# Feed-forward tiles turned by transposing DMAs, PSUM taken two banks at a time, weights transposed by numpy

## The reference, cut to what matters

```python
# x (4, 512, 512) float32, 2048 tokens of D = 512; token_ids choose one of 4 experts; ctx (4, 512, 512) holds their weights
h = layernorm(x)
for e in range(4):                       # only the tokens of expert e keep its y
    g = silu(h @ ctx[e].T); u = h @ ctx[e].T        # Wg = Wu = Wd = ctx
    y = (g * u) @ ctx[e].T
x1 = x + tanh(g_xattn[0]) * y
def bit_linear(x, w, b):                 # x rounded to 8 bits by its row's largest value, w to -1, 0, 1
    gamma_x = clip(max(abs(x), -1), 1e-5);  x_dq = clip(round(x * 127 / gamma_x), -128, 127) * gamma_x / 127
    gamma_w = clip(mean(abs(w)), 1e-5);     w_dq = clip(round(w / gamma_w), -1, 1) * gamma_w
    return x_dq @ w_dq.T + b
n = layernorm(x1)
z = silu(bit_linear(n, gate_w, gate_b)) * bit_linear(n, val_w, val_b)      # hidden size H = 2048
out = x1 + tanh(g_ffn[0]) * bit_linear(z, out_w, out_b)
```

## Time and profile before

| | |
|---|---|
| median of 3 runs | 369.0 us (368.78 to 369.78) |
| the profiled execution | 367.59 us, of which its span in the profile is 365.5 us |
| stage 1, up to the first expert product | 0 to 24 us |
| stage 2, expert units | 24 to 165 us |
| stage 3, feed-forward | 165 to 365.5 us |
| PE busy | 328.6 us (90%) |
| DVE busy | 294.5 us (81%) |
| POOL busy | 259.4 us (71%) |
| ACT busy | 229.5 us (63%) |
| granted TensorE clock, mean | 0.984 of full speed |

### The profile page before, as it was taken

The page is one execution under the profiler, slowest core; times in us unless marked ns, Lnnn a source line. Parts: engine busy times, 40 slices in busy tenths (PEclk is TensorE's granted clock), DMA queues, the critical chain, the costliest instruction groups (busy, mean ns, idle before and its releaser), DMA issues.

```text
span 365.5 us, 7169 instructions
## 1 busy us (share of the span) xinstructions
PE 328.6 (90%) x1976; PEld 177.8 (49%) x1992; DVE 294.5 (81%) x644; ACT 229.5 (63%) x327; POOL 259.4 (71%) x306
## 2 busy tenths in 40 slices
PE   2858899989998999789779999999999999999972
PEld 2734455546565555454335455544555455554440
DVE  5874777767787866788999899998999889998760
ACT  2837474657874456474467776687766877668650
POOL 2470366568878887847887888888888888888711
PEclk9979999999999999999999999999999999999997
DMA  6969257569312227231101101111011110110011
GB/s 244 302 225 388 57 208 266 179 203 248 126 58 65 84 84 275 70 89 34 32 2 29 59 31 58 58 30 58 29 58 55 31 58 29 59 47 11 29 39 49
DMA packets 24598, 37.03 MB, mean 101 GB/s; under 512 B 4543, under 2 KB 12735, under 8 KB 24320
## 3 DMA queue, kind: packets, MB, share of 16 engines
q1 hardware_dynamic: 20256, 23.38, 20.4%
q0 software_dynamic: 4320, 13.40, 10.6%
HBM read 28.35 MB, written 9.20 MB: 103 GB/s over the span
## 4 chain that ended last, share of the span: by engine, by line
PE 51%; POOL 17%; issue 10%; DVE 10%; DMA 6%; ACT 4%; POOLq 1%; SPq 0%; ACTq 0%; DVEq 0%
PE bank L587 25%; PE bank L605 15%; POOL raw L349 6%; PE bank L503 4%; PE bank L595 4%; POOL x_sb L331 3%; ACT tern L705 2%; POOL xg L302 2%; DMA x_rows<-x_sb,scatter_at 2%; POOL rstd L331 2%; DMA raw<-in_ctx 2%; POOL x_rows L315 1%; PE bank L469 1%; POOL var_eps L328 1%; POOL raw L388 1%
## 5 line engine op out<-in xcount | busy, mean ns | idle before, releaser
L587 PE MATMUL bank<-tern,raw 128*128 128x512 bf16 x512 | 118.2, 379 | 1.0 <-DVE raw L1042 0.7
L388 POOL TENSOR_TENSOR raw<-raw 128x512 f32<-128x512 f32 x63 | 80.3, 1278 | 21.5 <-ACT raw L776 18.1
L503 PE MATMUL bank<-w_hi,turned 128*128 x304 | 73.8, 386 | 9.1 <-DVE turned L915 7.9
L587 PEld LDWEIGHTS bank<-tern,raw 128*128 (+1 forms) x512 | 48.7, 98 | 55.3 <-ACT raw L761 1.3
L776 ACT ACTIVATE raw<-raw 128x512 f32<-128x512 f32 x64 | 39.9, 624 | 47.8 <-DVE raw L1042 46.3
L605 PE MATMUL bank<-tern,raw 128*128 128x512 bf16 x241 | 57.1, 379 | 3.7 <-ACT raw L780 1.9
L1042 DVE SCALAR_TENSOR_TENSOR raw<-bank,raw 128x512 f32<-128x512 f32 x64 | 47.6, 744 | 6.1 <-PE bank L587 5.4
L1050 DVE SCALAR_TENSOR_TENSOR raw<-bank,raw 128x512 f32<-128x512 f32 x64 | 47.6, 744 | 3.0 <-POOL raw L388 0.9
L503 PEld LDWEIGHTS bank<-w_hi,turned 128*128 128x128 f16 x304 | 29.8, 98 | 38.9 <-issue 13.8
L768 ACT ACTIVATE raw<-raw,magic 128x1024 f32 (+1 forms) x32 | 39.2, 1235 | 6.7 <-DVE raw L1069 6.7
L713 ACT ACTIVATE sign_sb<-raw,magic 128x1024 bf16<-128x1024 f32 (+1 forms) x24 | 27.2, 1148 | 25.9 <-POOL raw L349 25.7
(11 more groups left out here) (115 smaller groups left out, 477.4 us busy)
## 6 DMA issues: line engine op xcount, KB each, us to landing
raw<-x_rows SPq DMA_DIRECT2D x16, 257.5 KB, 2.6
raw<-in_ctx SPq DMA_DIRECT2D x4, 1024.0 KB, 8.2
raw<-in_L_ffn_gate_w SPq DMA_DIRECT2D x4, 1024.0 KB, 9.8
raw<-in_L_ffn_val_w SPq DMA_DIRECT2D x4, 1024.0 KB, 5.1
raw<-in_L_ffn_out_w SPq DMA_DIRECT2D x16, 256.0 KB
raw<-in_L_ffn_gate_b SPq DMA_DIRECT2D x1, 1024.0 KB
raw<-in_L_ffn_val_b SPq DMA_DIRECT2D x1, 1024.0 KB
xg<-in_x,gather_at POOLq DMA_INDIRECT x19, 3.8
```

The source lines that it names most:

```text
L388: nc.gpsimd.tensor_tensor(flat(z[:, bass.ds(t % 2, 1), c * D:(c + 1) * D]), s_post[:, c % 2, :], v_pre[:, c % 2, :], ALU.mult).then_inc(z_ ...
L503: last = nc.tensor.matmul(acc[:, :], a[:, k * P:(k + 1) * P], flat(w[:, bass.ds(e4 + k, 1), :]), start=(k == 0 and i == 0), stop=(k == KD ...
L587: last = nc.tensor.matmul(ps[c % 2][:, :].rearrange("p (a b) -> p a b", b=P), flat(xiT[:, bass.ds(t % 2, 1), k * P:(k + 1) * P]), rhs, sta ...
```

## The change

- The host lays out the expert matrices and the three weight matrices transposed, each as 128 rows of contiguous data. The 64 expert transposes, and `turn_pair` with `keep_pair` for the 24 pairs, are gone. `w_high` and `w_low` work on pairs of 128x1024 straight from the loaded data in SBUF, all on ACT and DVE, and `sign_pair` writes `tern` directly. Each expert gets at least one unit of slots.
- Rounding begins two slots earlier (`W_SLOT` 6 in place of 8), and three tiles are loaded early in place of two (`EARLY`).
- x and z are turned by `dma_start_transpose` on SP's queue, from SBUF to SBUF: one of 128x512 for each tile's x and two of 128x1024 for its z. `x_keep`, `z_keep` and the PE transposes of stage 3 are gone.
- The gate has two places of two PSUM banks, the value one place of two banks. `gate` and `val` run 8 matmuls into 128x1024, and `pre_gate`, `pre_val`, silu, POOL's multiply (`z_pair`) and `z_max` take 1024 columns at a time, in two chunks for each tile.
- The second half of `unshift_z` moves from POOL to ACT. x of tile `t + 2` in place of `t + 1` is prepared in slot `t`.
- z and its rounded and turned forms lie where the expert weights were (`w_both`), so POOL waits for the last expert product before the first `z_pair`.
- The loops of SP, POOL and DVE over the tiles are written out. PE and ACT keep theirs.

```diff
-    EARLY = 2
+    XR = 8
+    EARLY = 3
     BEFORE_EARLY = UNITS - 3
-    W_SLOT = 8
+    W_SLOT = 6
...
-        w_hi = sb("w_hi", [P, E * KD, D], f16)
-        w_lo = sb("w_lo", [P, E * KD, D], f16)
+        w_both = sb("w_both", [P, E * KD * D], f32)
+        w_hi, w_lo = (w_both[:, i * E * KD * D // 2:(i + 1) * E * KD * D // 2].bitcast(f16).rearrange("p (n d) -> p n d", d=D)
+                      for i in range(2))
...
+        g_sb = area(2 * 2 * D).rearrange("p (b d) -> p b d", b=2)
...
+        xiT = area(D, bf16).rearrange("p (b k m) -> p b k m", b=2, m=P)
...
+        area = areas_of(w_both[:, :])
+        z = area(2 * H).rearrange("p (b d) -> p b d", b=2)
         zq = area(H)
         zi = area(H // 2, bf16)
         ziT = area(H // 2, bf16).rearrange("p (h m) -> p h m", m=P)
...
-        g_ps, v_ps = bank[0:2], bank[2:4]
-        ziT_ps = wT_ps
-        xiT_ps = bank[6][:, :].bitcast(bf16)[:, 0:D]
-        o_ps = bank[7]
+        g_ps = (banks[:, 4:6, :], banks[:, 0:2, :])
+        v_ps = banks[:, 6:8, :]
+        o_ps = bank[2]
...
+                if n == 8:
+                    sp.wait_ge(whi_made, E * KD // 2)
+                    sp.wait_ge(wlo_made, E * KD // 2)
+                w = (gate_w, val_w, out_w)[m]
+                sp.dma_start(flat(raw[:, m * G + 4 * q:m * G + 4 * q + 4, :]), w[:, q * H:(q + 1) * H]).then_inc(raw_loaded[n], 16)
...
+            def turn_x(t):
+                sp.wait_ge(xi_made, t + 1)
+                if t >= 2:
+                    sp.wait_ge(v_done, 2 * (t - 1))
+                sp.dma_start_transpose(xiT[:, t % 2, :, :], xi).then_inc(x_turned, 16)
...
+            def turn_z(t, half):
+                sp.wait_ge(zi_made[half], t + 1)
+                if t >= 1:
+                    sp.wait_ge(z_read[half], t)
+                sp.dma_start_transpose(ziT[:, half * G // 2:(half + 1) * G // 2, :],
+                                       zi[:, half * H // 2:(half + 1) * H // 2]).then_inc(z_turned[half], 16)
...
+            turn_x(0)
+            turn_x(1)
...
+            for t in range(TILES + 1):
+                if 3 <= t < TILES - 1:
+                    load_tokens(t + 1)
+                if t >= 1:
+                    turn_z(t - 1, 0)
+                    turn_z(t - 1, 1)
+                if t + 2 < TILES:
+                    turn_x(t + 2)
+                if t + XT < TILES:
+                    load_rows(t + XT)
...
+            def unshift_z(t):
+                pool.wait_ge(zq_made[0], t + 1)
+                if t >= 1:
+                    pool.wait_ge(z_turned[0], 16 * t)
+                nc.gpsimd.tensor_scalar(zi[:, 0:H // 2], zq[:, 0:H // 2], magic[:, 1:2], one[:, 0:1],
+                                        ALU.add, ALU.mult).then_inc(zi_made[0], 1)
+            def z_pair(t, c, width=2 * D):
+                pool.wait_ge(s_made, 2 * t + c + 1)
+                pool.wait_ge(v_made, 2 * t + c + 1)
+                nc.gpsimd.tensor_tensor(z[:, t % 2, 2 * D * c:2 * D * c + width], g_sb[:, c, 0:width],
+                                        v_sb[:, c, 0:width], ALU.mult).then_inc(z_made, 1)
...
+            pool.wait_ge(bias_scaled, 1)
             add_bias(0)
             add_bias(1)
...
+            pool.wait_ge(y_done, UNITS)
+            for t in range(TILES):
+                if t >= 1:
+                    z_pair(t - 1, 1)
+                if t >= 3:
+                    store(t - 3)
+                if 1 <= t < TILES - 1:
+                    add_bias(t + 1)
+                if t >= 1:
+                    unshift_z(t - 1)
+                z_pair(t, 0)
+            z_pair(TILES - 1, 1, D)
+            for t in range(TILES - 3, TILES):
+                store(t)
...
+            def gate(t, c, start=False):
+                n = 2 * t + c
+                if not start:
+                    pe.wait_ge(g_made, n - 1)
+                for b in range(2):
                     for k in range(KD):
...
+            def val(t, c, start=False):
+                n = 2 * t + c
+                if not start:
+                    pe.wait_ge(v_made, n)
+                for b in range(2):
+                    for k in range(KD):
+                        last = nc.tensor.matmul(v_ps[:, b, :], flat(xiT[:, bass.ds(t % 2, 1), k, :]),
+                                                tern[:, G + k * HC + 2 * c + b, :], start=(k == 0), stop=(k == KD - 1))
+                last.then_inc(v_done, 1)
...
+                pe.wait_ge(z_turned[half], 16 * (t + 1))
                 if half == 0 and start:
+                    pe.wait_ge(signed, PAIRS)
+                    pe.wait_ge(gu_made, UNITS)
                 elif half == 0:
                     pe.wait_ge(o_made, t)
                 for k in range(half * G // 2, (half + 1) * G // 2):
...
+                    last = nc.tensor.matmul(o_ps, ziT[:, k, :], tern[:, 2 * G + k, :],
                                             start=(k == 0), stop=(k == G - 1))
+                    if k == G // 2 - 1:
+                        last.then_inc(z_read[0], 1)
...
+            def ffn_slot(t, downs=True, start=False, start_down=False):
+                pe.wait_ge(x_turned, 16 * (t + 1))
+                gate(t, 0, start)
+                val(t, 0, start)
+                if downs:
                     down(t - 2, 0, start_down)
+                gate(t, 1, start)
+                val(t, 1)
+                if downs:
                     down(t - 2, 1)
...
+            pe.wait_ge(signed, G)
+            ffn_slot(0, downs=False, start=True)
+            ffn_slot(1, downs=False)
             ffn_slot(2, start_down=True)
             with pe.Fori(3, TILES - 1) as t:
                 ffn_slot(t)
...
+            t = TILES - 1
+            pe.wait_ge(x_turned, 16 * (t + 1))
+            gate(t, 0)
+            val(t, 0)
+            gate(t, 1)
+            val(t, 1)
+            for t in range(TILES - 3, TILES):
+                down(t, 0)
                 down(t, 1)
...
+            def w_high(p):
+                if p % 2 == 0:
+                    act.wait_ge(ctx_loaded[p // 2], 16)
+                nc.scalar.activation(flat(w_hi[:, 2 * p:2 * p + 2, :]), flat(raw[:, 2 * G + 2 * p:2 * G + 2 * p + 2, :]),
+                                     ACT.Copy, scale=W_SCALE).then_inc(whi_made, 1)
+            for p in range(E * KD // 2):
+                w_high(p)
...
+                nc.scalar.activation(flat(tern[:, bass.ds(2 * p, 2), :]), flat(raw[:, bass.ds(2 * p, 2), :]), ACT.Sign,
...
+            def unshift_z(t, start=False):
+                act.wait_ge(zq_made[1], t + 1)
+                if not start:
+                    act.wait_ge(z_turned[1], 16 * t)
+                nc.scalar.activation(zi[:, H // 2:H], zq[:, H // 2:H], ACT.Identity, bias=magic[:, 1:2]).then_inc(zi_made[1], 1)
...
+            def silu_gate(t, c):
+                act.wait_ge(g_made, 2 * t + c + 1)
+                nc.scalar.activation(g_sb[:, c, :], g_sb[:, c, :], ACT.Silu).then_inc(s_made, 1)
...
+            def ffn_slot(t, before=True, start=False, after=True):
+                silu_gate(t, 0)
                 if before:
...
+                    z_round(t - 1, 1, start)
+                    unshift_z(t - 1, start)
+                silu_gate(t, 1)
+                if after:
+                    x_round(t + 2)
+                    x_unshift(t + 2)
...
+            def w_low(p):
+                dve.wait_ge(whi_made, p + 1)
+                v.scalar_tensor_tensor(flat(w_lo[:, 2 * p:2 * p + 2, :]), flat(raw[:, 2 * G + 2 * p:2 * G + 2 * p + 2, :]), W_SCALE,
+                                       flat(w_hi[:, 2 * p:2 * p + 2, :]), ALU.mult, ALU.subtract).then_inc(wlo_made, 1)
...
+            for t in range(TILES):
+                pre_gate(t, 0)
+                if t >= 1:
+                    z_max(t - 1, 1)
+                    z_max_both(t - 1)
                     z_gamma(t - 1)
                     z_scales(t - 1)
+                pre_val(t, 0)
+                if t + 2 < TILES:
+                    tile_norm(t + 2)
+                    x_max(t + 2)
+                    x_gamma(t + 2)
+                pre_gate(t, 1)
+                if t + 2 < TILES:
+                    x_scales(t + 2)
                 z_max(t, 0)
...
+                pre_val(t, 1)
+                if 2 <= t < TILES - 1:
+                    finish(t - 2)
...
+            t, last = TILES - 1, slice(D, 2 * D)
+            dve.wait_ge(s_made, 2 * TILES)
+            dve.wait_ge(v_made, 2 * TILES)
+            v.tensor_tensor(z[:, t % 2, H - D:H], g_sb[:, 1, last], v_sb[:, 1, last], ALU.mult).then_inc(z_last, 1)
+            finish(t - 2)
+            dve.wait_ge(z_last, 1)
+            z_max(t, 1)
+            z_max_both(t)
+            z_gamma(t)
+            z_scales(t)
+            finish(t - 1)
+            for half in range(2):
+                dve.wait_ge(zq_made[half], TILES)
+                dve.wait_ge(z_turned[half], 16 * t)
```

(10 more changed lines are left out.)

588 lines of the change are left out of this document (130 added, 458 removed).

## The result

The changed kernel takes 393.8 us (median of 4 runs, 393.27 to 393.99) against 368.9 us of the kernel before on the same chip (4 runs, 367.34 to 369.78): ratio 1.068, 95% interval 1.064 to 1.072. The prediction was 380.6 us and its range ended at 392. The direction was right. The loss is 24.9 us where 11.6 were predicted.

A forecast was written before the change was run, and what follows sets the result against it. A ring through POOL, DVE and ACT was taken to bound stage 3: 177.2 + 15 x 11.92 = 356.0, plus a 21.1 us tail, is a span of 377.1, +11.6 us, so a median of 380.6 us; range 361 to 392.

The forecast's parts named there:

- H(0): End of pre_val(0, 1), the first tile's second value chunk in stage 3, predicted at 177.2 us.
- The tail: From the last tile's pre_val(15, 1) to the end of the kernel: 21.1 us.
- the ring: Stage 3's once-a-tile path from one pre_val(t, 1) to the next through POOL, DVE and ACT: 11.92 us, bounds 11.2 to 12.6.
- The bound: Steady stage 3: the ring sets the tile period, PE waits for DVE's pre_val and is busy near 87%.
- Prices of 1024 columns: Stage 3 operations scaled from two widths: POOL's multiply 2.37 us, DVE's reduction 1.19, DVE's scale-and-add 1.27.
- Stage 1: Up to slot 1: at most 1.5 us gained at the first product, then taken back; sum 0, bounds -1.5 and +1.
- Stage 2: Expert slots: earlier rounding +2.1 us, two more early DMAs some 0.9, yet the last scatter at 169.0 us, bounds 167 and 172.
- The +2.1 us of `W_SLOT`: Rounding in slots 5 and 6 makes them cost 2 x 7.6 = 15.2 us in place of 13.08.
- The start of stage 3: After the last scatter at 169.0: two add_bias, then first z_pair, z_max and pre_val, ending at 177.2 us.
- The transposing DMAs: SP's queue in stage 3: 3.8 us for half a z, 1.9 for x, 9.5 a tile, hidden under 11.9.
- H(15): End of pre_val(15, 1), the last tile's second value chunk, predicted at 356.0 us after fifteen tiles of 11.92.
- The removal: PE's transposes removed in stage 3: PE idles some 1.5 us a tile, so removing them buys nothing.

The follow-up runs named there:

- e1_pool_order: The changed kernel with z_pair(t, 0) ahead of unshift_z(t - 1) in POOL's loop: 376.8 us.
- e2_plain_dma: The changed kernel with its transposing DMAs of x and z replaced by plain DMAs of the same bytes, on untransposed data: 390.8 us.
- e6_no_hold: The changed kernel with z_scales' product as a tensor_scalar and tile_norm from tile 2 on written to PSUM: 387.5 us.
- e14_low_first: The kernel of e6_no_hold with x1, gu_low and bn_stats of the last two units ahead of tile_norm(0) on DVE: 387.0 us.
- e3_warm_pe: The changed kernel with useless matmuls on PE: 20 during the wait for the last unit's gu_low, 26 before the last down product: 390.4 us.
- e7b_before_noturn: The kernel before, with PE's transposes of x and z left out from tile 3 on except the last of each group: 364.2 us against 368.7.
- e9_tokens_late: The kernel of e5_val_first with the token load behind the tile's transposes and load_rows in SP's loop: 378.6 us.
- e5_val_first: The changed kernel with POOL's z_pair(t, 0) and unshift_z ahead of store and add_bias, and DVE's pre_val(t, 0) ahead of z_max(t-1, 1): 388.4 us.

## Why the prediction was right and wrong

**In short.** The direction and the mechanism, a ring through POOL, DVE and ACT that the written orders close, were right. Three terms of the sum were too small. The start stands first: the last scatter, put at 169.0, came at 173.03, and a hold of 2.5 us behind it was left out, so H(0) was 183.7 and not 177.2. The tail was 25.5 us and not 21.1, and the ring 12.20 us and not 11.92.

**The bound.** Right. The ring through POOL, DVE and ACT sets the period, PE waits for `pre_val`, and PE is busy 87%, as written. e1_pool_order shows the ring and e2_plain_dma excludes the DMAs from it.

**Prices of 1024 columns.** Right: multiply 2.36 us (2.37 predicted), scale-and-add 1.27 to 1.28 (1.27), reduction 1.22 (1.19). Scaling by the column from two widths of one operation held in all three.

**The ring.** 11.92 us predicted, 12.20 on average and 12.3 in the middle, within its bounds. 0.25 us is DVE's operations held by POOL, shown by e6_no_hold. The prediction had this mechanism and put it in its bound of 12.6, not in the sum, although had shown it. It looked for it at the unshift alone. The rest, about 0.1 us, is in the hand-overs.

**Stage 1.** Sum 0 predicted. The scatter of slot 5 is at 67.22, 1.26 us later than in the earlier trace rows and 0.26 outside the bound. It is nearly all there by the first scatter (48.40 against 47.22), and 0.77 us of it by the first expert product (24.91 against 24.14), where the prediction had expected a gain. I did not isolate which of its new orders costs this.

**Stage 2.** The +2.1 us of `W_SLOT` came exactly: from slot 5 to slot 15 it is 75.95 us against 73.86, and the slots are 7.6 us apart. But the step failed at its last line. Having found +2.1 and +0.9 us, I took the last scatter as 0.5 us earlier than before (169.0), on the ground that the last slots hang on other engines and on round trips. Those begin where the rounding slots end, and the round trip carries the delay on. SP's early loads wait for earlier scatters and started at 158.11, where they had started at 154.64. The scatter of unit 16 waits for their landing and came at 164.28, where it had come at 159.66. Of these 4.6 us, 3.5 are the delay and 0.95 the two DMAs of the third tile. `x1` of the last unit waits for that scatter to land and for the last product, which ended at 169.37 and not near 165.2. From the scatter of slot 15 to the last one it is 29.86 us, against 29.68 in the earlier trace rows. An early last product alone isn't the cure: in e14_low_first it ended at 163.54, and H(0) moved by 1.0 us. 169.50 + 1.26 + 2.1 + 0.2 = 173.03. This is 4.0 of the 6.5 us of the start.

**The start of stage 3.** The steps from the last scatter to H(0) sum to 8.2 us, which e6_no_hold measured. In the changed kernel it was 10.7, and the missing term is the hold of `tile_norm(2)` by two `add_bias` and the multiply, 2.5 us. It lies at a place where the earlier trace rows showed the mechanism for a single POOL operation (1.42 us). With three of them back to back it lasts until the last of them ends.

**The transposing DMAs.** 3.8 and 1.9 us taken, 3.1 and 2.5 measured from issue to landing, hidden in the steady part. The bound from the plain DMA in the earlier trace rows was the better end. The figure of the Trainium skill, 1309 ns for a block of 128x128 (VectorE: DVE Perf Modes, "The three transpose paths"), can't be taken per block in a row: eight blocks landed in 3.1 us. PE's 219 ns beside it are the duration of one transpose; the 192 of the earlier trace rows kept PE busy for only 14.6 us. The rule of the Trainium skill that transposes by DMA are as fast as plain ones (Advanced Engine Details and Errata, "X-Bar Transpose (TRN2)") is nearer: 3.1 against 2.3 us here.

**The tail.** 21.1 us predicted, 25.5 measured. `finish(14)` ended at H(15) + 6.9 us, not 5.65, as `down(14)` waited for its own transposes. From the issue of the last transposes to the end of the last product it was 374.25 to 385.49, 11.2 us, where the sum had 7.5: both halves arrived before PE started (4.8 us), and then the product ran at the lower clock. e3_warm_pe puts the clock at 2.8 us of that. The prediction took 1.8 us for the second half's `down` from matmuls that ran at 2.4 GHz and hid the first half's behind the second transpose. It never asked what the idle time that it had itself found ahead of them, up to the landing of the transposes, would do to the clock. Its terms up to `finish(15)` add up to 14.6 us, not 14.65, which changes nothing.

**The removal.** The sentence that the removed transposes buy nothing was nearly right for a reason that I had not seen: e7b_before_noturn gives them 4.5 us, since POOL's unshift stood 0.2 us behind in the kernel before.

**The range.** It ended at 392 with a span sum of 377.1. Three terms of 4.2 to 6.5 us, all in the same direction, were missed. The chance for the direction (0.75) stood on the ring, which was well founded; the range of its time stood on the ring's bounds alone, and the start and the tail had none in it above their sums.

## What to carry to other kernels

When work moves off the engine that bounds a kernel, write down the next closed path through the other engines' orders before counting the gain; one was 0.2 us behind here. Merging two half-width steps into one adds nothing to the engines' sums and nearly doubles each link of such a path (POOL's multiply 1.27 us at 512 columns, 2.36 at 1024). No run goes back to 512 columns, so that the width made the ring the bound is argued and not shown. What is shown is that the order of two lines can take a link out: 17 us of 25 came back without any change of work. A delay at the end of one stage goes into the next one whole, unless a wait there is shown to have room for it.

## What the runs showed of the hardware

- A VectorE product of two inputs in SBUF was held until GpSimd's operation ended, though it has one column: 0.73 us in the changed kernel and 0.83 in e9_tokens_late, in place of 0.14 (370.52 in the changed kernel). As a tensor_scalar with the second column as its scalar it took 0.20 us beside the same GpSimd operation.
- A normalisation of 128x512 from SBUF to SBUF was held through three GpSimd operations in a row, 4.71 us. With its output in PSUM it took 0.81 us and was not held; alone, in SBUF, it took 0.54. So writing to PSUM cost 0.27 us here and removed the hold.
- GpSimd's multiply of 128x1024 took 2.53 us when it started beside a normalisation from SBUF to SBUF (251.93), 2.36 otherwise.
- After 6.2 us without work TensorE ran 16 matmuls in 6.44 us, at 3.63 after 26 matmuls without use. At the start the last expert product took 2.76 us in place of 5.30 in the same way, and H(0) didn't move, since `x1` behind it then waited for a scatter to land.
- SP's queue issued two transposes of 128x1024 in 2.6 us (242.92 in e5_val_first). What stands ahead of them in the written order counts too: one token load ahead of them cost e5_val_first 9.9 us.
